# Last attention of an eight-stage kernel: narrow chunks of two head pairs in one slot, and an order from a list scheduler

## The reference

```python
q, k, v = split(x @ W_attn + b_attn)              # each [B=4, H=16, T=1024, hd=8]
q, k = rope(q), rope(k)                           # angle by head index
att = q @ k^T / sqrt(8); att[masked] = -inf
y = softmax(att) @ v
x = x + (y @ W_proj + b_proj)
```

## Time and profile before

| | us |
|---|---|
| median of 3 runs | 3105.89 (3104.85 to 3114.9) |
| profiled execution: its time | 3092.15 |
| profiled execution: its span | 3090.4 |
| last attention in it, first search to last projection | about 2475 to 3012 |

### The profile page before, as it was taken

How to read it: one execution, slowest core, us unless ns; L and a number is a source line. 1 busy time by engine, 2 the same in 40 slices (tenths; PEclk the granted TensorE clock), 3 DMA queues, 4 the chain that set the end, 5 groups by cost and what they waited for, 6 DMA issues and landing times.

```text
span 3090.4 us, 54695 instructions
## 1 busy us (share of the span) xinstructions
PE 2638.1 (85%) x20224; PEld 1714.0 (55%) x20224; DVE 2038.8 (66%) x4696; ACT 1696.9 (55%) x3346; POOL 912.4 (30%) x995
## 2 busy tenths in 40 slices
PE   7999899988998899678998668788766988888879
PEld 4666666665666567664446536666665622323325
DVE  5566556555665564258874248999997887777735
ACT  4776466645664566241212237877862446666662
POOL 1000020002000200443223466777875122322221
PEclk9999999999999999799999788899998989999999
DMA  5000000000000000220002111122222520110000
GB/s 181 2 2 2 1 10 2 2 1 10 2 2 1 10 2 21 62 59 18 9 9 59 48 49 62 63 70 68 71 76 85 180 97 2 56 56 2 2 2 28
DMA packets 79944, 114.24 MB, mean 37 GB/s; under 512 B 10109, under 2 KB 48172, under 8 KB 79680
## 3 DMA queue, kind: packets, MB, share of 16 engines
q1 hardware_dynamic: 71488, 97.07, 9.6%
q0 software_dynamic: 8192, 13.67, 1.6%
HBM read 77.66 MB, written 35.78 MB: 37 GB/s over the span
## 4 chain that ended last, share of the span: by engine, by line
PE 26%; issue 11%; DVE 10%; POOL 8%; another core or an unknown queue 3%; ACT 1%; DVEq 0%; POOLq 0%; SPq 0%; ACTq 0%
POOL arena L2083 6%; DVE Wqkv L2354 5%; PE ps L2230 4%; PE ps L1385 3%; PE ps L1191 3%; PE ps L688 3%; PE ps L677 2%; PE ps L2202 2%; PE ps L2191 1%; PE ps L1394 1%; PE ps L2195 1%; PE ps L1182 1%; PE ps L2239 1%; POOL arena L2066 1%
## 5 line engine op out<-in xcount | busy, mean ns | idle before, releaser
L387 ACT ACTIVATE arena<-ps 128x512 f32<-128x512 f32 (+1 forms) x640 | 333.9, 548 | 406.1 <-PE ps L291 392.3
L499 DVE CUSTOM_DVE_ANT_0 arena<-ps,causal 128x512 f32<-128x512 f32 (+3 forms) x512 | 282.2, 588 | 323.7 <-PE ps L278 286.4
L400 ACT ACTIVATE arena<-arena 128x640 f32<-128x640 f32 (+7 forms) x512 | 394.3, 771 | 37.8 <-DVE arena L499 34.1
L2354 DVE TENSOR_REDUCE Wqkv<-ps 128x2 f32<-128x1024 f32 (+3 forms) x384 | 353.1, 953 | 86.6 <-PE ps L2195 81.3
L2310 ACT ACTIVATE arena<-ps 128x1024 f32<-128x1024 f32 (+3 forms) x384 | 302.1, 809 | 162.6 <-PE ps L2202 158.9
L291 PE MATMUL ps<-ident,arena 128*128 128x128 f32 x2304 | 345.8, 283 | 46.3 <-ACT arena L400 31.9
L2083 POOL TENSOR_TENSOR arena<-arena,W 128x1024 f32<-128x1024 f32 x128 | 332.6, 2618 | 133.8 <-DVE W L2035 133.8
L1791 PE MATMUL ps<-rope,arena 128*128 128x128 f32 x2048 | 282.2, 300 | 96.2 <-ACT rope L1930 48.1
L291 PEld LDWEIGHTS ps<-ident,arena 128*128 128x128 f32 x2304 | 254.3, 142 | 161.7 <-issue 87.5
L312 PE MATMUL ps<-arena,rope 128*64 128x128 f32 x4608 | 341.5, 284 | 0.0
L1791 PEld LDWEIGHTS ps<-rope,arena 128*128 128x128 f32 x2048 | 267.9, 213 | 126.3 <-issue 72.0
(11 more groups left out here) (265 smaller groups left out, 4272.3 us busy)
## 6 DMA issues: line engine op xcount, KB each, us to landing
select<-c_rows SPq DMA_DIRECT2D x64, 512.0 KB, 3.6
arena<-q_dram SPq DMA_DIRECT2D x4, 2048.0 KB, 9.0
arena<-k_dram SPq DMA_DIRECT2D x4, 2048.0 KB, 14.2
q_dram<-arena SPq DMA_DIRECT2D x24, 256.0 KB, 3.7
k_dram<-arena SPq DMA_DIRECT2D x24, 256.0 KB, 3.8
arena<-slots_in SPq DMA_DIRECT2D x8, 640.0 KB, 6.6
slots_out<-arena SPq DMA_DIRECT2D x8, 640.0 KB, 4.3
slots_in<-select SPq DMA_DIRECT2D x4, 640.0 KB, 6.3
```

The source lines that it names most:

```text
L387: nc.scalar.activation(k.probT[:, n % 2, b0 * P:(b0 + nb) * P], k.ps[:, 4 + m % 2, 0:nb * P], ACT.Copy)\
L400: nc.scalar.activation(k.prob[:, i % 2, h, 0:w], k.prob[:, i % 2, h, 0:w], ACT.Exp, bias=k.neg_max[:, i % 2, h:h + 1], scale=-1.0, accum_o ...
L499: ins = nc.vector.tensor_tensor_reduce(k.prob[:, i % 2, h, 512 * g:512 * g + w], k.ps[:, banks[h], 0:w], k.causal[:, first:first + w], 1.0 ...
L2354: nc.vector.tensor_reduce(k.least[:, g, a, i % 4, c, :], k.ps[:, 2 * (m % 3):2 * (m % 3) + 2, 0:search_width(i, c)], AX_X, ALU.min)\
```

## The change

Two things are changed, both inside this stage.

First, chunks of at most 256 columns are no longer done pair by pair. Both pairs of such a chunk are written side by side into one slot (pair a at columns a * w), and one DVE minimum, one ACT exponential and one POOL cut take all of it. PE's matmuls are the same in number and size. 128 of the 384 searches become 64, and likewise 128 of the 384 weighs and of the 256 cuts 128 become 64. Other chunks stay as they were.

Second, `b_order` and all fixed places give way to `b_plan`, a list scheduler that runs when the program is built. At each step it lists the kinds that could go next (search, weigh, values, maxima, outputs, epilogue) with the time at which each could start by a small table of costs, keeps those within 100 ns of the soonest, and takes the one with the lowest rank: maxima first, then outputs and epilogue, then search or weigh by how little work their reader has left, values last. A search or weigh takes the slot that comes free first. All engines walk the plan in its order. Searching may run at most four groups ahead of weighing.

```diff
-B_LEAD = 32
-EPILOGUE = (9, 13, 17, 21)
+def pairs_in_unit(w):
+    return ((0, 1),) if w <= 256 else ((0,), (1,))
+B_SLOTS = 3
+def b_plan():
+    hop, drain = 100, 180
...
+    while len(searched) < len(B_SEARCH) or len(valued) < len(B_STEPS) or outputs or epilogues:
...
+        free = min(slots) + hop
+        if S < len(B_SEARCH):
+            ahead = W < len(B_WEIGH) and b_group(*B_SEARCH[S][:3]) > b_group(*B_STEPS[B_WEIGH[W][0]][:3]) + 4
+            if not ahead:
+                ready.append((max(now, free, searched[-2] + hop if S >= 2 else 0), dve - now, "search"))
...
+            if group in row and V >= s - 1:
+                ready.append((max(now, free, row[group] + hop, exped[-3] + hop if W >= 3 else 0), act - now, "weigh"))
...
+            ready.append((max(now, at + hop), 1300, "values"))
...
+        soonest = min(ready)[0]
+        start, _, kind = min((r for r in ready if r[0] <= soonest + 100), key=lambda r: r[1])
+        slot = slots.index(min(slots))
+        if kind == "search":
+            now = start + max(100, 2 * len(As) * w // 5) + 100 + 200 * (c == i // 4)
+            dve = max(dve, now + drain + hop) + 60 + 2 * len(As) * w * 21 // 20
...
+        elif kind == "weigh":
+            now = start + max(100, 2 * len(As) * w // 5) + 50
+            act = max(act, now + drain + hop, valued[s - 2] + hop if s >= 2 else 0) + 90 + 2 * len(As) * w * 41 // 50
...
+        elif kind == "values":
+            now = start + 9 * weigh_span(g, j)[1] // 5 + 100
...
+            row[group] = sp + 2500
...
 # PE, search and weigh
-            mm = nc.tensor.matmul(k.ps[:, 2 * slot + h, 0:w], ...)
+        for at, a in enumerate(As):
+            for h in range(2):
+                mm = nc.tensor.matmul(k.ps[:, 2 * slot + h, at * w:(at + 1) * w], ...)
 # PE, the loop
-    for m, (kind, n) in enumerate(B_ORDER):
-        wait_slot(pe, sm, m)
+    for kind, n, slot, before in B_PLAN:
         if kind == "search":
+            wait_slot(pe, sm, before)
...
 # ACT
-            nc.scalar.activation(k.expT[:, n % 4, :, 0:w], k.ps[:, 2 * (m % 3):2 * (m % 3) + 2, 0:w], ACT.Exp, scale=-1.0)
+            nc.scalar.activation(k.expT[:, at:at + len(As), :, 0:w],
+                                 k.ps[:, 2 * slot:2 * slot + 2, 0:len(As) * w].rearrange("p h (a w) -> p a h w", w=w),
+                                 ACT.Exp, scale=-1.0).then_inc(sm["exp"], 1)
 # DVE
-            nc.vector.tensor_reduce(k.least[:, g, a, i % 4, c, :],
-                                    k.ps[:, 2 * (m % 3):2 * (m % 3) + 2, 0:search_width(i, c)], AX_X, ALU.min)
+            nc.vector.tensor_reduce(k.least[:, g, As[0]:As[-1] + 1, i % 4, c, :],
+                                    k.ps[:, 2 * slot:2 * slot + 2, 0:len(As) * w].rearrange("p h (a w) -> p a h w", w=w),
+                                    AX_X, ALU.min).then_inc(sm["searched"], 1)
 # POOL
-                nc.gpsimd.affine_select(out=k.expT[:, n % 4, :, 0:P], ..., pattern=[[0, 2], [1, P]], ...)
+                part = k.expT[:, at:at + len(As), :, 0:P].rearrange("p u h c -> p (u h) c")
+                nc.gpsimd.affine_select(out=part, in_=part, ..., pattern=[[0, 2 * len(As)], [1, P]], ...)
```

More of the change, by code:

```diff
@@ L2114, in weigh_span @@
     return first, 512 * (g + 1) - first
[L2117 to L2137, removed]
+def pairs_in_unit(w):
+    return ((0, 1),) if w <= 256 else ((0,), (1,))
+B_SEARCH = [(b, Q, g, i, c, As) for b in range(NB) for Q in range(4) for g in range(2) for i in range(4 * g, 4 * g + 4)
+            for c in range(g + 1) for As in pairs_in_unit(search_width(i, c))]
+B_STEPS = [(b, Q, g, j) for b in range(NB) for Q in range(4) for g in range(2) for j in range(4 * g + 4)]
+B_WEIGH = [(s, As) for s, (b, Q, g, j) in enumerate(B_STEPS) for As in pairs_in_unit(weigh_span(g, j)[1])]
+B_SLOTS = 3
 def b_group(b, Q, g):
     return 8 * b + 2 * Q + g
-def b_group_searched(group):
-    return 24 * (group // 2) + (8, 24)[group % 2]
-B_AUX = {B_ORDER.index(("search", b_group_searched(group) - 1)) + 5: group for group in range(8 * NB)}
 def b_group_done(s):
@@ L2156, in b_group_done @@
     return b_group(b, Q, g) if j == 4 * g + 3 else None
[L2159 to L2173, removed]
+B_SEARCHED = {b_group(b, Q, g): n + 1 for n, (b, Q, g, i, c, As) in enumerate(B_SEARCH)}
+B_WEIGHED = {s: n + 1 for n, (s, As) in enumerate(B_WEIGH)}
@@ L2174, in wait_slot @@
+B_PLAN = b_plan()
+def wait_slot(eng, sm, before):
+    if before is not None:
+        kind, n = before
         eng.wait_ge(sm["searched" if kind == "search" else "exp"], n + 1)
@@ L2257, in epilogue @@
             mm.then_inc(sm["y_ps"], 1)
-    for m, (kind, n) in enumerate(B_ORDER):
-        wait_slot(pe, sm, m)
+    for kind, n, slot, before in B_PLAN:
         if kind == "search":
-            b, Q, g, a, i, c = B_SEARCH[n]
-            if n % 96 == 0:
+            b, Q, g, i, c, As = B_SEARCH[n]
+            wait_slot(pe, sm, before)
+            if n == 0 or B_SEARCH[n - 1][0] != b:
                 pe.wait_ge(sm["stack%d" % b], 16 * 2)
-            search(m % 3, b, Q, a, i, c)
-        else:
[L2267 to L2282, removed]
+            search(slot, b, Q, i, c, As)
+        elif kind == "weigh":
+            s, As = B_WEIGH[n]
+            b, Q, g, j = B_STEPS[s]
+            wait_slot(pe, sm, before)
+            if j == 0 and As[0] == 0:
+                pe.wait_ge(sm["max_row%d" % g], 32 * (b_group(b, Q, g) // 2 + 1))
+            weigh(slot, b, Q, g, j, As)
+        elif kind == "values":
+            values(n)
+        elif kind == "outputs":
+            outputs_to_tokens(n)
+        elif kind == "epilogue":
+            epilogue(*n)
+        else:
+            maxima_to_rows(n)
     pe.wait_ge(sm["x_new"], 2 * NB)
@@ L2301, in take_rows @@
         nc.scalar.activation(flat(k.out_bT[:, 4 * half:4 * half + 4, :]), k.ps[:, 7, :], ACT.Copy).then_inc(sm["attT"], 1)
-    for m, (kind, n) in enumerate(B_ORDER):
+    for kind, n, slot, _ in B_PLAN:
         if kind == "weigh":
-            b, Q, g, j, a = B_WEIGH[n]
+            s, As = B_WEIGH[n]
+            b, Q, g, j = B_STEPS[s]
             w = weigh_span(g, j)[1]
+            at = (2 * s + As[0]) % 4
             act.wait_ge(sm["weigh_ps"], n + 1)
[L2308 to L2324, removed]
+            if s >= 2:
+                act.wait_ge(sm["value_ps"], s - 1)
+            nc.scalar.activation(k.expT[:, at:at + len(As), :, 0:w],
+                                 k.ps[:, 2 * slot:2 * slot + 2, 0:len(As) * w].rearrange("p h (a w) -> p a h w", w=w),
+                                 ACT.Exp, scale=-1.0).then_inc(sm["exp"], 1)
+        elif kind == "values" and b_group_done(n) is not None:
+            take_output(b_group_done(n))
+        elif kind == "epilogue" and n[1] < 2:
+            take_rows(*n)
+        elif kind == "maxima":
+            act.wait_ge(sm["nmT_ps"], n + 1)
+            if n >= 2:
+                act.wait_ge(sm["max_row%d" % (n % 2)], 32 * (n // 2))
+            nc.scalar.activation(k.nmT[0:32, n % 2, :], k.ps[0:32, 7, :], ACT.Copy).then_inc(sm["nmT"], 1)
 def dve_attention_b(nc, k, dve, ch, sm):
@@ L2360, in dve_attention_b @@
                     .then_inc(sm["least"], 1)
[L2361 to L2368, removed]
+        elif kind == "outputs":
+            normalize(n)
+        elif kind == "epilogue" and n[1] >= 2:
+            add_result(n[0], n[1] - 2)
     dve.wait_ge(sm["x_new"], 2 * NB)
@@ L2373, in pool_attention_b @@
     split_done = 0
-    ends = {b_group_searched(group): group for group in range(8 * NB)}
     pool.wait_ge(f1["xn2"], CHUNKS)
-    for kind, n in B_ORDER:
+    for kind, n, _, _ in B_PLAN:
         if kind == "weigh":
-            b, Q, g, j, a = B_WEIGH[n]
+            s, As = B_WEIGH[n]
+            b, Q, g, j = B_STEPS[s]
             if j >= 4 * g:
+                at = (2 * s + As[0]) % 4
+                part = k.expT[:, at:at + len(As), :, 0:P].rearrange("p u h c -> p (u h) c")
                 pool.wait_ge(sm["exp"], n + 1)
[L2381 to L2384, removed]
+                nc.gpsimd.affine_select(out=part, in_=part, compare_op=ALU.is_ge, fill=0.0, base=0,
+                                        pattern=[[0, 2 * len(As)], [1, P]], channel_multiplier=-1).then_inc(sm["cut"], 1)
+            if (Q, g, j, As[0]) == (0, 1, 2, 0):
                 X = k.X_all[:, 8 * b:8 * b + 8, :]
```

139 lines of the change are left out of this document (109 added, 30 removed).

## The result

| | before | changed |
|---|---|---|
| median of 5 runs, us | 3104.85 (3103.71 to 3114.9) | 3062.09 (3058.16 to 3079.38) |
| profiled execution: its time, its span | 3092.15, 3090.4 | 3079.38, 3077.3 |
| stage, first search until DVE has added the last projection, in it | 2475.5 to 3011.6: 536.1 | 2502.6 to 2999.4: 496.8 |

The changed kernel takes 0.9871 of the time of before (95% interval 0.9848 to 0.9894), 40 us less by the ratio. The forecast was 3072 us, 34 less. The profiled execution is the slowest of its five: its stage begins 27 us later than in before, in code that the change does not touch. So the stage is compared by its own length, 39.3 us less.

What follows compares the result with a forecast made beforehand. Three slots handed round, neither side alone, bound the stage; 2499 + 383 + 45 + 8 + 2 + 41 = 2978 against 3012, 34 us less, gives 3105.9 - 34 = 3072 us. Forecast range 3051 to 3086, 8 in 10 from 3031 to 3103.

Steps and rivals of the forecast that it cites:

- The bound: Whole stage: three slots handed round, neither side the bound alone; PE holds 421 us and waits 86 in the middle.
- The merge: Narrow chunks: saves 10 us of DVE, 11 of ACT, 0 of POOL; above all 768 slot turns become 640.
- The head: First search to first weigh: 4 us won, as the row of maxima lands at about 2499 behind the stacks.
- the 8 us for the clock: After the first weigh: 8 us of half-clock loss where before had 4, after PE idles for 9 us.
- The middle: First weigh to last search: 383 us of PE work plus waits of 45, 8 for the clock and 2 for groups 1 and 3.
- the turns short of PE work: Middle: too little PE work before a slot refills; 152 turns by 60.3 us against 256 by 99.6, giving 50 us of waits.
- The tail: Weighs after the last search: ACT and POOL set the pace, merged exponentials save 1 us, leaving 41.
- The sums: Stage end: 2499 + 383 + 45 + 8 + 2 + 41 = 2978 against 3012, 34 us less.
- a middle that waits 6 us: Fast end of the 8-in-10 range: 75 us less, 3031.
- A: Rival: only the reader's savings pay, 10 us less DVE work gives 13.5 us, the order nothing: 3092; chance 0.20.
- B: Rival: the plan works as meant, waits of 10 us in the middle, 70 us less, 3036; chance 0.15.
- C: Rival: plan prices about 25 us short of PE's, PE comes late, middle waits 108 us, 3135; chance 0.15.

Runs made afterwards that it cites:

- The kernel with the rows first: Changed kernel with SP issuing the stacks of sequence 1 after the rows of maxima of groups 0 and 1: stage 486.7 us, ratio 0.9832 to before.
- either half of the merge: Changed kernel with only searches merged, or only weighs merged: stages 503.1 and 502.8 us, ratios 0.9877 and 0.9882 to before.
- the other prices: The kernel with the rows first, its plan made with PE prices read from the trace: stage 486.3 us against 486.7, ratio 0.9832 to before.
- values first: Changed kernel, its plan made with values at rank -400 instead of 1300: stage 518.6 us, ratio 0.9948 to before.
- Cheaper minima: Before and changed kernel, minima of 384- or 512-key chunks over the first 256 keys only: stages 498.4 and 490.8 us, ratios 0.9846 and 0.9845.

## Why the prediction was right

- The bound. Three slots are handed round, and PE is held for 421 us of 536 in before and 415.5 in the changed kernel: nothing in the runs speaks against it. All kernels of the table have the same 3936 matmuls in this stage, and what differs in the main is how long PE waits.
- The merge. 10 and 11 us of reader time were priced to the row (1.223, 0.690, 1.024). That nothing is saved on POOL was wrong: 64 cuts at 0.634 are 11 us less. What they are worth in time no run shows; POOL is busy for 132 us of the stage. "What the merge does above all is take away slot turns" is not enough as it stands: with the old list 128 fewer turns bring nothing, with the plan 21.5 us.
- The head. 4 us forecast, 5 measured, for the reason given: the row lands with the stacks, PE stands 10.58 us. The kernel with the rows first shows the reason directly, and the 10 us that the forecast put on it. One step of the head failed: the 8 us for the clock were put on PE's standing, and with the rows first, where PE hardly stands, the granted clock behind the first weigh is the same 0.79 and the middle as long.
- The middle. 383 us of work and 55 of waiting were forecast, 438; it lasts 433, that is 50 of waiting. The number was right, but the step that gave it, waits in proportion to the turns short of PE work, is not what sets them. Scaled on before in the same way, it missed by 13 us with the merge alone (527 against 539.9), by 7.5 with the plan alone, by 5 with either half of the merge, by 4 with the other prices, and by 22 with values first, where it even has the wrong sign. That it came within 5 us for the changed kernel was luck, as far as the runs show.
- The tail. 41 forecast, 41.4 measured.
- The sums. They hold but for small things: the middle of before lasts 465.4 us, not 467, and a middle that waits 6 us gives 73 us less, not 75. Neither moves the forecast.
- The rivals. A fell: the merge alone, with some 10 us less work for DVE, gives nothing (1.0015), and the plan alone, without it, gives 17.6 us. Beside it stood the rule of the Trainium skill ("Perfetto Trace Analysis", Identifying the Most-Contended Engine) to treat the fullest engine first. The runs bear it out in part: 118 us less for DVE at the wide chunks give the old list 38 us, 10 us less at the narrow ones give it nothing. DVE's work does count, but its busy share does not tell where. B's 10 us of waiting was not reached: 47 remain. C fell with the corrected prices.

What stands in place of the failed step, as far as the runs show it: in the old list PE waits mostly at a weigh behind a search, for a slot that DVE still reads (59 of 80 us of gaps lie between a search or its mask and a weigh). They are at the wide chunks: by the list, which says whose slot it is, about 40 of these 59 us go to slots of searched 512-key chunks and 10 to those of 384 keys. DVE takes 1.22 us for the first and 0.95 for the second. Some 8 us more are for slots that ACT reads. Cheaper minima take 33 us of waiting away in before, and 5 from the plan. The plan has cut these gaps to 10 us. What remains in the changed kernel lies in the main at the searches behind weighs (28 of 47 us), where ACT holds the slot.

Which part of the plan cuts the gaps stays open. It is not the low rank of values, since with values first the gaps are still only 16 us; that rank saves another wait, the one of values for their exponential, which the old list hardly had either (3 us). The choice by how little work a reader has left, the place of the first weighs (13 slot turns in instead of 33), and the slot that comes free first were not tested one by one; the last matters little by the count, since 581 of 637 turns take the slot that rotation would give. Why the merge of narrow chunks needs the plan to pay is only argued too: in the old list the turns it frees lie where PE was not waiting, and only a free order can spend them at the wide chunks. No run placed the freed turns by hand.

## What to carry to other kernels

Where buffers are handed round between one producer and two readers, and both sides wait for each other, a busy share does not say what a saving is worth; ask at which piece of work the producer stands, and for whom. A piece that needs a reader's result (values here) must not be placed so early that the producer stands for that result: ranked last it cost nothing there, ranked first 22 us. A merge of small units is worth testing together with the order, for alone it may bring nothing (here nothing and 17.6 us alone, 39 together). And a small transfer that starts a phase must not be queued behind a large one that nobody needs yet: one moved call gave 10 us.

## What the runs showed of the hardware

- Two 6 KB DMAs, of which SP issued the first 0.6 us behind 4 MB, were waited for until 12.8 us after that issue. Without the 4 MB ahead of them they were waited for until 2.8 us after.
- GpSimd's cut of 128x512 takes 0.634 us and of 128x256 0.406. As an estimate from these two, 256 more columns cost 0.23 us and 0.18 is fixed.
- The clock granted behind the first weigh is 0.79 over 36 us in the plan's order, with 10 us of standing ahead of it or without, and 0.95 in the old order.
- The changed program's profiled executions span 3077.3 us on one chip and 2954.7 on another, while this stage differs by 0.2 us. The difference lies ahead of it: its first search starts 123 us later.
